# Local attentions: the mask added by VectorE instead of TensorE, and the shared expert's first blocks ahead of the counts

## What is computed

```python
q, k = l2norm(q) * qs, l2norm(k) * ksc
q, k = rotary_xpos(q, k)
sim = einsum('bhwid,bhwjd->bhwij', bq * 8.0, bk)        # windows of 64, the one before included
mask = (i < j) | (i > j + WINDOW) | (j == -1)
attn = softmax(where(mask, -max, sim))
x = x + (attn @ bv) @ wo
```

```python
topk_p, topk_i = top_k(softmax(norm(x) @ router_w.T), 2)
routed = scatter_add(expert rows * weights)             # first 320 tokens of each expert
shared = silu(x @ sg) * (x @ su) @ sd
return shared + routed
```

## Time and profile before

| what | value |
|---|---|
| time before, median of 3 runs | 1694.15 us (1691.04 to 1697.17) |
| the profiled execution's own time | 1694.25 us |
| its span, first to last instruction | 1692.5 us |
| granted TensorE clock, mean | 0.937 |
| PE busy | 1485.3 us, 88% |
| a middle batch of a local attention, from one minus_top (L916) of ScalarE to the next (152.59 to 172.87) | 20.28 us |
| the same for the first batches (85.28 to 111.99, 300.88 to 321.00) | 26.71 and 20.12 us |
| the same for the seventh batches (213.42 to 231.69, 422.43 to 440.70) | 18.27 us each |
| DVE, ACT, POOL busy | 1009.6, 855.5, 672.6 us |

### The profile page before, as it was taken

How to read it: one execution, slowest core, us unless ns; L and a number is a source line. 1 busy time by engine, 2 the same in 40 slices (tenths; PEclk the granted TensorE clock), 3 DMA queues, 4 the chain that set the end, 5 groups by cost and what they waited for, 6 DMA issues and landing times. The chain is left out here.

```text
span 1692.5 us, 30745 instructions
## 1 busy us (share of the span) xinstructions
PE 1485.3 (88%) x11059; PEld 1089.7 (64%) x11059; DVE 1009.6 (60%) x2372; ACT 855.5 (51%) x1876; POOL 672.6 (40%) x779
## 2 busy tenths in 40 slices
PE   4689999899987999996939999999998799969996
PEld 3356676566764667675827877878878467635554
DVE  6656646666477799994035555366655322456665
ACT  5456555655548877772424443544444323235552
POOL 3387716877132777872130000100003532223434
PEclk8799999999998999997859999999999799979998
DMA  7300000000204777626234000000000010200000
GB/s 213 104 14 14 13 14 1 14 13 17 91 1 60 86 79 80 80 40 139 66 95 131 1 1 1 1 1 1 0 1 1 29 54 16 66 4 2 2 2 26
DMA packets 80944, 66.58 MB, mean 39 GB/s; under 512 B 28283, under 2 KB 67243, under 8 KB 80815
## 3 DMA queue, kind: packets, MB, share of 16 engines
q1 hardware_dynamic: 71198, 57.24, 17.4%
q0 software_dynamic: 2688, 5.53, 1.1%
q10 hardware_dynamic: 6928, 2.12, 0.6%
HBM read 48.89 MB, written 11.71 MB: 36 GB/s over the span
## 5 line engine op out<-in xcount | busy, mean ns | idle before, releaser
L1557 POOL TENSOR_TENSOR inject<-delta_x,b_rows 128x512 f32<-128x512 f32 x128 | 160.1, 1277 | 63.9 <-DVE delta_x L1854 37.6
L1881 DVE TENSOR_TENSOR_SCAN state<-bank,inject 128x512 f32<-128x512 f32 x128 | 150.2, 1211 | 7.5 <-issue 5.2
L2314 POOL TENSOR_TENSOR ve<-mv,eps 128x1 f32<-128x1 f32 x32 | 6.1, 190 | 335.4 <-DVE mv L2462 335.4
L1786 ACT ACTIVATE bank<-delta,a_neg 128x255 f32<-128x255 f32 x256 | 109.1, 472 | 7.5 <-DVE state L1881 6.6
L2423 ACT ACTIVATE Z<-bank 128x512 f32<-128x512 f32 x64 | 34.7, 594 | 129.2 <-PE bank L2376 129.2
L2400 ACT ACTIVATE U<-bank 128x512 f32<-128x512 f32 x128 | 74.7, 593 | 40.4 <-PE bank L2337 39.3
L632 POOL TENSOR_TENSOR rotated<-rot_cos,rot_sin 128x512 f32<-128x512 f32 x52 | 65.8, 1269 | 47.1 <-DVE rot_sin L1001 47.1
L1661 PEld LDWEIGHTS bank<-tabs,by_token 128*128 128x128 f32 x512 | 68.3, 197 | 24.9 <-issue 15.1
L3618 DVE TENSOR_REDUCE top<-bank 128x2 f32<-128x512 f32 (+1 forms) x96 | 61.4, 686 | 30.3 <-PE bank L3322 16.9
L638 POOL TENSOR_TENSOR inv_norm<-sum_sq,neghalf 128x16 f32<-128x16 f32 x26 | 76.1, 2926 | 3.9 <-POOL sum_sq L636 0.8
L1797 ACT ACTIVATE by_token<-bank,c_cols 128x256 f32<-128x256 f32 x128 | 53.6, 470 | 46.3 <-PE bank L1635 46.0
(11 more groups left out here) (575 smaller groups left out, 4138.3 us busy)
## 6 DMA issues: line engine op xcount, KB each, us to landing
b_rows<-rows_dram SPq DMA_DIRECT2D x32, 512.0 KB, 8.9
v<-v SPq DMA_DIRECT2D x32, 130.0 KB, 2.4
by_token<-zero SPq DMA_DIRECT2D x8, 256.0 KB, 3.3
moe_w<-in_L_ffn_rg_dram SPq DMA_DIRECT2D x1, 2048.0 KB, 8.6
moe_w<-in_L_ffn_ru_dram SPq DMA_DIRECT2D x1, 2048.0 KB, 13.8
x_with_id<-by_token SPq DMA_DIRECT2D x16, 128.0 KB, 2.3
wqkv<-in_L_ffn_wqkv_dram SPq DMA_DIRECT2D x2, 768.0 KB
rows<-padded SPq DMA_DIRECT2D x5, 258.0 KB, 4.2
```

The lines of the kernel that those rows point to most:

```text
L1557: pool.tensor_tensor(dB[:, n % R, :, :], dx[:, :, seq(n)], both(b_all[:, q % 4, n % CH, :]), ALU.mult).then_inc(s.inject.sem, 1)
L1786: last = act.activation(dA[n % RD][:, c, 1:L], delta[:, c, i * L + 1:(i + 1) * L], ACT.Exp, scale=a_neg[:, c, k:k + 1])
L1881: dve.tensor_tensor_scan(flat(h[:, n % R, :, :]), flat(dA[n % RD]), flat(dB[:, n % R, :, :]), 0.0, ALU.mult, ALU.add).then_inc(s.state.sem, 1)
```

## The change

In the local attentions the two mask products at the head of each score block go. VectorE adds the mask instead: `mask_scores` reads a bank S[y] of finished scores and the bf16 mask and writes the sum into `prob` in SBUF; ScalarE takes the exponential there in place. TensorE's next block now waits for VectorE's pass (`masked`) instead of for the exponential. On VectorE the first two passes stand behind the first rotation, the last two behind the second, ahead of everything else of the turn.

In the experts the shared expert's first pair of batches starts at the head of the stage. TensorE does its blocks 0 and 1 ahead of the counts; VectorE's eight products of the pair are laid between its steps on slots and weights; ScalarE copies the tokens behind the second Silu, and takes the exponential of the weights behind the first Silu of the second pair.

```diff
@@ local attention, TensorE @@
         def shifted(i, p, r):
             if r == 0:
                 pe.wait_ge(s.top_row.sem, s.top_row.at(i, 1))
-            for y in range(2):
-                pe.wait_ge(s.exped.sem, s.exped.at(i, r * (y + 1)))
-                pe.matmul(S[y], net.ident16[:, :], net.lmask16[:, 0:L].unsqueeze(1).to_broadcast([P, 2, L]), start=True, stop=False)
             for e in range(2):
                 c = 2 * r + e
                 for y in range(2):
-                    pe.matmul(S[y][:, e * L:(e + 1) * L], pick[row(y), c:c + 1].to_broadcast([LDH, P]), top_row[row(y), :], start=False, stop=False)
+                    if e == 0:
+                        pe.wait_ge(s.masked.sem, s.masked.at(i, r * (y + 1)))
+                    pe.matmul(S[y][:, e * L:(e + 1) * L], pick[row(y), c:c + 1].to_broadcast([LDH, P]), top_row[row(y), :], start=(e == 0), stop=False)
@@ local attention, ScalarE @@
         def exp(i, r):
             for y in range(2):
-                act.wait_ge(s.shifted.sem, s.shifted.at(i, 2 * r + y + 1))
-                act.activation(prob[:, 2 * r + y, :], S[y], ACT.Exp, scale=QK_SCALE).then_inc(s.exped.sem, 1)
+                of = prob[:, 2 * r + y, :]
+                act.wait_ge(s.masked.sem, s.masked.at(i, 2 * r + y + 1))
+                act.activation(of, of, ACT.Exp, scale=QK_SCALE).then_inc(s.exped.sem, 1)
@@ local attention, VectorE @@
+        def mask_scores(i, r):
+            for y in range(2):
+                by_query = lambda ap: ap.rearrange("p (e q) -> p e q", e=2)
+                dve.wait_ge(s.shifted.sem, s.shifted.at(i, 2 * r + y + 1))
+                dve.tensor_tensor(by_query(prob[:, 2 * r + y, :]), by_query(S[y]), net.lmask16[:, 0:L].unsqueeze(1).to_broadcast([P, 2, L]), ALU.add)\
+                    .then_inc(s.masked.sem, 1)
...
             if ahead >= 2:
                 rotate(dve, i + 2, 0)
+            mask_scores(i, 0)
+            if ahead >= 2:
                 rotate(dve, i + 2, 1)
+            mask_scores(i, 1)
             if mlp:
                 mlp(-2)
@@ experts, TensorE @@
-                pe.wait_ge(s.tables.sem, s.tables.at(0, 1))
-                pe.wait_ge(s.hot.sem, s.hot.at(0, 1))
-                flat = hot[:, :, :].rearrange("p e t -> p (e t)")
-                pe.matmul(bank[2][:, 0:NT * E2], ones[:, :], flat, start=True, stop=True)
-                pe.matmul(bank[1][:, 0:NT * E2], before[:, :], flat, start=True, stop=True).then_inc(s.counts.sem, 1)
+                def count():
...
                 def shared_expert(first, end):
                     for i in range(first, end):
                         for c in range(SC):
+                            if i == 0 and c == 2:
+                                count()
@@ experts, ScalarE @@
-                for half in range(2):
-                    for c in range(2):
...
-                act.wait_ge(s.shifted.sem, s.shifted.at(0, 1))
-                act.activation(gap[:, :], gap[:, :], ACT.Exp).then_inc(s.exp.sem, 1)
+                def number_rows():
...
+                            if i == 0 and c == 1:
+                                number_rows()
+                            if i == 1 and c == 0:
+                                act.wait_ge(s.shifted.sem, s.shifted.at(0, 1))
+                                act.activation(gap[:, :], gap[:, :], ACT.Exp).then_inc(s.exp.sem, 1)
@@ experts, VectorE @@
                 dve.tensor_tensor(hot[:, :, :], hots[:, 0, :, :], hots[:, 1, :, :], ALU.add).then_inc(s.hot.sem, 1)
+                shared_pair(0, 0, 2)
...
                 counts_before(dve, link, pre[:, :, :], keep[:, :, :], bank[1][:, 0:NT * E2], bank[2][:, 0:NT * E2])
+                shared_pair(0, 2, 4)
...
                 dve.tensor_tensor(scatter[:, :, :], offset[:, :, :], trash, ALU.add).then_inc(s.slots.sem, 1)
+                shared_pair(0, 4, SC)
...
-                for i in range(FIRST):
+                for i in range(1, FIRST):
                     shared_pair(i)
```

More of the change, by code:

```diff
@@ L539 @@
 LOCAL_SPEC = ("settled:0 clear:1 tables:4 h_built:1 qk_ps:4 squared:4 sums:4 clipped:4 inv_norm:4 sind:4 added:4 roped:4 "
[L540 removed]
+              "turned:4 qk16:4 qkT:4 v_ps:2 v_ready:2 v_mid:32 scored:4 maxed:4 top16:1 top_parts:1 top_ps:1 top_row:1 shifted:4 masked:4 exped:4 "
               "mixed:4 row_inv:4 o_ready:4 oT_ps:2 oT_ready:2 y_ready:1 x_updated:1 ")
@@ L2857, in _ @@
                 pe.wait_ge(net.ld_w3, net.w3_ready)
-                pe.wait_ge(s.tables.sem, s.tables.at(0, 1))
-                pe.wait_ge(s.hot.sem, s.hot.at(0, 1))
-                flat = hot[:, :, :].rearrange("p e t -> p (e t)")
-                pe.matmul(bank[2][:, 0:NT * E2], ones[:, :], flat, start=True, stop=True)
-                pe.matmul(bank[1][:, 0:NT * E2], before[:, :], flat, start=True, stop=True).then_inc(s.counts.sem, 1)
+                def count():
+                    pe.wait_ge(s.tables.sem, s.tables.at(0, 1))
+                    pe.wait_ge(s.hot.sem, s.hot.at(0, 1))
+                    flat = hot[:, :, :].rearrange("p e t -> p (e t)")
+                    pe.matmul(bank[2][:, 0:NT * E2], ones[:, :], flat, start=True, stop=True)
+                    pe.matmul(bank[1][:, 0:NT * E2], before[:, :], flat, start=True, stop=True).then_inc(s.counts.sem, 1)
                 def shared_down(p):
@@ L2930, in _ @@
             def _(act):
-                for half in range(2):
-                    for c in range(2):
-                        of = net.x_tok[:, half * T // 2:(half + 1) * T // 2].rearrange("p (t d) -> p t d", d=D)
-                        act.activation(with_id[:, c, half * NT // 2:(half + 1) * NT // 2, 0:D], of, ACT.Copy).then_inc(s.with_id.sem, 1)
-                act.wait_ge(s.shifted.sem, s.shifted.at(0, 1))
-                act.activation(gap[:, :], gap[:, :], ACT.Exp).then_inc(s.exp.sem, 1)
+                def number_rows():
+                    for half in range(2):
+                        for c in range(2):
+                            of = net.x_tok[:, half * T // 2:(half + 1) * T // 2].rearrange("p (t d) -> p t d", d=D)
+                            act.activation(with_id[:, c, half * NT // 2:(half + 1) * NT // 2, 0:D], of, ACT.Copy).then_inc(s.with_id.sem, 1)
                 def keep_shared(i):
@@ L2994, in link, with shared_pair @@
                     dve.wait_ge(s.v.sem, s.v.at(0, count[0]))
+                def shared_pair(i, first=0, end=SC):
+                    for c in range(first, end):
+                        dve.wait_ge(s.s_silu.sem, s.s_silu.at(i, c + 1))
+                        dve.wait_ge(s.su_ps.sem, s.su_ps.at(i, c + 1))
+                        if i >= 2:
+                            dve.wait_ge(s.shared_ps.sem, s.shared_ps.at(2 * (i - 1), 0))
+                        dve.tensor_tensor(shid[:, i % 2, c, :], sgate[:, c % 2, :], up_bank(c)[:, :], ALU.mult).then_inc(s.s_hid.sem, 1)
                 count_tables(dve, link, net, before[:, :], ones[:, :], keep[:, :, :], E2)
@@ L3028, in _ @@
                 weights()
-                def shared_pair(i, first=0, end=SC):
-                    for c in range(first, end):
-                        dve.wait_ge(s.s_silu.sem, s.s_silu.at(i, c + 1))
-                        dve.wait_ge(s.su_ps.sem, s.su_ps.at(i, c + 1))
-                        if i >= 2:
-                            dve.wait_ge(s.shared_ps.sem, s.shared_ps.at(2 * (i - 1), 0))
-                        dve.tensor_tensor(shid[:, i % 2, c, :], sgate[:, c % 2, :], up_bank(c)[:, :], ALU.mult).then_inc(s.s_hid.sem, 1)
-                for i in range(FIRST):
+                for i in range(1, FIRST):
                     shared_pair(i)
```

1 line of the change is left out of this document (removed).

## The result

| | before | after |
|---|---|---|
| time, median | 1694.37 us (1691.04 to 1697.17, 4 runs) | 1712.60 us (1711.77 to 1719.23, 4 runs) |
| ratio, 95% interval | | 1.0124 (1.0110 to 1.0138) |
| profiled execution, its span | 1694.25, 1692.5 | 1712.12, 1710.3 |
| PE, DVE, ACT busy | 1485.3, 1009.6, 855.5 | 1482.4, 1053.9, 859.6 |
| granted clock, mean | 0.937 | 0.934 |

Slower, as forecast, but by more: 1707.2 was forecast, with a range of 1698 to 1715. By the ratio the changed kernel takes 1715.2 on the 1694.15 of before, just above the range; the median of its own four runs, 1712.60, lies inside.

What follows compares the result with a forecast made beforehand. It took TensorE, VectorE and ScalarE as three almost equally long chains in a batch. The terms +1.5 - 0.9 + 7.15 + 6.4 + 3.5 - 4.7 = +12.95 on 1694.25 gave 1707.2 us, range 1698 to 1715.

Steps and rivals of the forecast that it cites:

- the middle batches' +1.5: Ten middle batches of the local attentions: +0.15 us each from later projections, bounds -0.75 to +0.8 a batch.
- the clock's +3.5: TensorE's new stalls in first and last attention batches lower its granted clock to half: +3.5 us, bounds 0 and +8.
- the last batches' 0.7: Half clock after stalls of about 4 us in each attention's last batch, in half of the cases: together +0.7 us.
- The mask pass: VectorE's mask addition over a 128x512 bank: 0.69 us to the result, 0.60 to the next start; floor 0.42, ceiling 0.84.
- From there squares, the next two rotations and the last transposes are as before: Middle batches: after the projections, at 162.2 and 163.2, nothing more changes, so a batch costs +0.15 us.
- Seventh batches: Seventh batch of each attention: no rotations on VectorE, TensorE 0.45 us ahead; -0.9 us for two.
- First batches: First batch of each attention: masks queue behind a rotation waiting for GpSimd, projections start later; +3.85 and +3.3 us.
- Last batches: Last batch of each attention: the MLP's first norm waits behind the mask passes, delaying the output product; +3.2 us each, +6.4 together.
- The experts: Experts' stage: shared expert's first pair fills TensorE's idle start, second pair starts earlier, moved work is covered; -4.7 us, bounds -3 and -6.
- The first (TensorE is the bound, 1670.9): Attentions: masks leave the bounding TensorE, 32 blocks make -18.7 us, with the expert's -4.7: 1670.9 us; chance 0.05.
- the second, a pass of 0.55 to 0.60: About the same: cheaper VectorE mask passes, middle batches -0.3 us each, no loss of clock; +4.4, 1698.7 us; chance 0.13.
- The third (1719.7): Worse: mask passes take 0.75 us, and ScalarE's copies and the slots eat the expert's gain; +25, 1719.7 us; chance 0.10.

Runs made afterwards that it cites:

- the double pass: Changed kernel with GpSimd waiting for the split row maxima, plus an unused same-size VectorE pass ahead of each mask pass; middle batches 22.93 us, one run.
- the experiment with GpSimd's wait: Changed kernel where GpSimd starts scaling the second half of rotated only after VectorE has split the row maxima; 1.0101 of the kernel before.

## Why the prediction was right in direction and short in size

The sum had +12.95 us, and the spans differ by 17.8. By its terms the miss is +3.8 in the middle batches, +2.7 in the last and +1.75 in the first ones (both with their clock), 0 from the seventh batches and the experts together, and -3.3 from places where nothing was edited. Two terms were mis-sized: the middle batches' +1.5, which measured +5.3, and the clock's +3.5, of which the last batches' 0.7 measured 3.3.

**The mask pass** was priced at 0.69 to the result and 0.60 to the next start. Measured: 0.684 in the mean of 64, pairs of 1.28. Right. ScalarE's exponential, taken as unchanged, has a mean of 0.629 us from SBUF against 0.595 from a bank; small.

**Middle batches: the step that failed.** Up to the projections the working was right within 0.03 us for masks, exponentials and projections, and the double pass confirms that all four passes lie on the way. The sentence that failed is "From there squares, the next two rotations and the last transposes are as before". Two things are in it. Without the collision the batch costs 0.22 us and not 0.15 (102.54 for five in the experiment with GpSimd's wait): 2.2 for ten instead of 1.5. And the working moved the work of VectorE and GpSimd by tenths of a microsecond against each other without a look at what stands side by side: the kernel before had at most 0.09 us between the splitting pass and GpSimd's multiplication. Once that was used up, eight of the ten batches lost a further 0.4: 3.1 us. Together +5.3 instead of +1.5. Both rows were in the trace of before, and neither is among those that the prediction reads.

**Seventh batches**: -1.3 for -0.9. Right.

**First batches**: the mechanism was right, and is shown by moving the masks or by leaving them to TensorE. From the rotation's sums (L1004) to the projections the first attention went from 2.91 to 7.81 us and the second from 3.47 to 7.80, so +4.9 and +4.3. The forecast had 3.85 and 3.3 with 1.6 and 1.2 of clock, 5.45 and 4.5: right within 0.6. The rest stands in front and behind. The sums come 0.8 and 1.2 us later against the minus_top row (10.56 to 11.34 and 5.65 to 6.88), and 0.1 and 0.3 are lost behind, one of these a splitting pass of 1.02 us. The 0.8 and 1.2 are not the change's: in the two profiles with unedited attentions (the experts' part alone) the sums stand at 10.79 and 11.36 in the first attention and at 6.89 in the second, and in the second profile of the changed kernel at 10.71 and 5.64. The two profiles on one chip, changed and unedited, differ by +9.9 in the two first batches (29.85 and 26.79 against 26.03 and 20.75), which is the forecast's 7.15 + 2.8; so the +11.7 of the first pair of profiles contains some 2 us of chance.

**Last batches**: here too the mechanism was right. The norm's start moved by 3.25 us against the minus_top row (from 234.75 - 231.69 = 3.06 to 244.09 - 237.78 = 6.31) for a forecast of 3.2. The rest of the +5.6 and +4.25, 2.3 and 1.0 us, is the clock's.

**The clock: the other term that was too small.** +3.5 was taken, with bounds 0 and 8, of which 0.7 for both last batches, as "half of the cases". They took 3.3. TensorE waited 3.86 us in both, and in both the granted clock was at half when the norm came: the output product took 3.62 and 3.04 us instead of 1.89. The waits of 10.32 and 4.79 us in the first batches ended in the same way. So not half of the cases but each of the four, and each of the twelve waits of 3.86 us in six profiles. How long the stretch then lasts is not fixed: 2.0 of the 2.65 us between two executions of the same program come of it. With the wait cut to 0.91 us the clock stayed at 1.00, in six of six last batches. The Trainium skill's rule that the forecast cited ("TensorE: Matmul & The Clock Gate", section "Part 1: The HAM clock gate") agrees in both directions.

**The experts**: -4.3 for -4.7. The second pair starts 4.4 us earlier against the last router product. Nothing waits for the rows. Right.

**Outside of the sum**: the stretch between scan and experts was 3.3 us shorter, with no edit in it. It hid part of the miss, and that the raw median still fell inside the range is luck of this kind; without it the change would have cost some 21 us. The -1.3, +0.3 and +1.0 at the other places without an edit are small beside it.

**The rivals.** The first (TensorE is the bound, 1670.9) is refuted, and not only by the result: even masks that cost nothing bring some 11 us in the attentions and not 18.7. Of the second, a pass of 0.55 to 0.60 was needed and 0.68 is measured. The third (1719.7) is nearer to the measured 1715.2 than the forecast, but by other means: passes of 0.75 and a lost gain of the experts, and neither happened.

## What to carry to other kernels

Taking work off the busiest engine pays only by what the next chains let through, and that can be worked out from one batch's rows; but then the order on the engines decides more than the price of the work. The same passes cost the attentions 21.5 to 26.5 us behind a waiting rotation, in front of a norm and with the exponentials in front of the copies. With these orders changed, GpSimd made to wait for the splits, and TensorE's own mask kept in the first batch, the attentions gained some 4 us. When work moves by tenths of a microsecond, look for pairs of VectorE and GpSimd passes that stand just beside each other, and ask whether the order in which they start survives. A result that is not needed soon (here the second exponentials) should not stand in front of a copy that frees a bank.

## What the runs showed of the hardware that was not expected

In the turns of the attentions a VectorE pass over 16 elements took 0.79 to 1.05 us when a GpSimd multiplication over 512 elements of SBUF had started 0.02 to 0.3 us ahead of it. It took 0.17 when GpSimd's started less than 0.014 us ahead or later, and also inside GpSimd's power pass of 2.92 us. The long passes recur in the same ten turns of the same program on two chips.

In the experts' stage some profiled executions have TensorE, ScalarE and VectorE idle with no releaser in the profile, TensorE for up to 9.23 us (the row at 1386.08). The stage then takes 177 to 190 us instead of 171 or 175.6. It is so in all seven profiles from two of the chips, with edited and unedited stages alike, and in none from the others, and its cause was not found; a comparison of totals across kernels is blurred by it, and the stages were compared instead.
